# A new prologue for a fused attention and expert layer: order of loads, where the weights' means and low halves are made, and new order tables

## The reference, cut to what matters

```
n   = (x - mean_c x) / sqrt(var_c x + eps)                    # norm over channels, per pixel
qkv = Wqkv n                                                  # 256 -> 768 channels
agg = Wpw (depthwise 5x5 of qkv)                              # pointwise in groups of 8 channels
o   = relu linear attention, 8 channels a head, of qkv and of agg
y   = x + BN(Wproj o)                                         # 512 -> 256 channels
t   = (y - mean_c y) / sqrt(var_c y + eps)
w   = expert weights from softmax(router mean_t t), top 2
out = y + sum_e w_e (W2_e gelu(W1_e t + b1_e) + b2_e)         # 6 experts, 256 -> 341 -> 256
```

## Time and profile before

| what | us |
|---|---|
| median of 3 runs (1475.28 to 1476.71) | 1475.31 |
| the profiled execution | 1477.36 |
| its span, first to last instruction | 1475.3 |
| TensorE products busy | 1360.7 (92%) |
| VectorE busy | 1242.8 (84%) |
| ACT busy | 1059.0 (72%) |
| GpSimd busy | 973.3 (66%) |
| mean granted TensorE clock | 0.978 of full speed |

### The profile page before, as it was taken

How to read it: one execution, slowest core, us unless ns; L and a number is a source line. 1 busy time by engine, 2 the same in 40 slices (tenths; PEclk the granted TensorE clock), 3 DMA queues, 4 the chain that set the end, 5 groups by cost and what they waited for, 6 DMA issues and landing times. The chain is left out here.

```text
span 1475.3 us, 18697 instructions
## 1 busy us (share of the span) xinstructions
PE 1360.7 (92%) x6844; PEld 778.3 (53%) x6844; DVE 1242.8 (84%) x1273; ACT 1059.0 (72%) x1887; POOL 973.3 (66%) x736
## 2 busy tenths in 40 slices
PE   5897788799999999999999999999999998999998
...
DVE  2998799999999999999999999999999999960100
...
DMA packets 14250, 32.74 MB, mean 22 GB/s; under 512 B 2384, under 2 KB 5328, under 8 KB 13904
## 3 DMA queue, kind: packets, MB, share of 16 engines
...
...
## 5 line engine op out<-in xcount | busy, mean ns | idle before, releaser
L1125 DVE SCALAR_TENSOR_TENSOR dacc<-qkvs,dww,dacc 128x960 f32<-128x960 f32 (+4 forms) x930 | 1026.7, 1184 | 0.0
L969 POOL TENSOR_TENSOR gl<-hb,gh 128x512 f16<-128x512 f32 x256 | 307.6, 1204 | 261.0 <-ACT hb L735 257.9
L939 POOL TENSOR_TENSOR dwo<-dwo,tapb 128x992 f32<-128x992 f32 (+2 forms) x100 | 230.7, 2307 | 83.6 <-ACT tapb L709 45.1
L833 ACT ACTIVATE hb<-wbk,b1s 128x512 f32<-128x512 f32 x256 | 174.0, 682 | 88.5 <-PE wbk L504 83.8
L517 PE MATMUL acc<-gh,w2h 128*128 128x512 f16 x512 | 195.0, 381 | 7.7 <-POOL gl L969 6.0
L517 PE MATMUL acc<-gl,w2h 128*128 128x512 f16 x512 | 194.9, 381 | 0.0
L517 PE MATMUL acc<-gh,w2l 128*128 128x512 f16 x512 | 194.7, 380 | 0.0
L734 ACT ACTIVATE gh<-hb,ew 128x512 f16<-128x512 f32 x256 | 182.9, 714 | 0.8 <-PE acc L517 0.2
L735 ACT ACTIVATE hb<-hb,ew 128x512 f32<-128x512 f32 x256 | 182.2, 712 | 0.0
L504 PE MATMUL wbk<-th,w1h 128*128 128x512 f16 x512 | 153.2, 381 | 8.0 <-ACT hb L833 2.0
L504 PE MATMUL wbk<-th,w1l 128*128 128x512 f16 x512 | 152.9, 380 | 0.0
...
## 6 DMA issues: line engine op xcount, KB each, us to landing
...
dwo<-w SPq DMA_DIRECT2D x1, 2048.0 KB, 14.5
...
```

The costliest lines, as they stand in the source:

```text
L833: last = nc.scalar.activation(hb[:, f % GB, :], b[:], ACT.Gelu, bias=b1s[:, f % FT:f % FT + 1], scale=1.0 / (X_SCALE * W_SCALE))
L939: ins = nc.gpsimd.tensor_tensor(d3[:, oy, ox], d3[:, oy, ox], t3[:, iy, ix], ALU.add)
L969: nc.gpsimd.tensor_tensor(gl[:, f % GB, :], hb[:, f % GB, :], gh[:, f % GB, :], ALU.subtract).then_inc(g_low, 1)
L1125: ins = nc.vector.scalar_tensor_tensor(out=dst[:, oy, ox], in0=i3[:, jy, jx], scalar=dww[:, m, tap:tap + 1], in1=a3[:, oy, ox], op0=ALU.mu ...
```

## The change

It changes the prologue and all five order tables.

1. SP loads image 0 first, then Wqkv; W1 and the router follow behind the batch norm's small vectors, and W2 moves to the end of the list.
2. The means of Wqkv go to the `acc` banks, and TensorE no longer waits for their subtraction before it goes on.
3. The means of W1 are made in four pieces of 512 columns (`means.0.0` to `means.0.3`), with a matrix `mean_s` of 64/256, and VectorE centres and scales each piece in one instruction as it comes. They still stand behind the norm's row in the order. ACT casts W1 in two halves behind the first qkv evictions.
4. The low halves of W1 and W2 are made by GpSimd (`w1l`, `w2l`, two instructions each) from weights that are already scaled; for W2 ACT writes the scaled f32 copy, two more activations. They are no longer a condition for the first tap; TensorE, ACT and VectorE wait for them where they need the result or the space.
5. VectorE waits for the norm's row (`ln_chain`) before it makes the low half of Wqkv. The reciprocals stand ahead of the centring of W1, the mask of Wpw behind it.
6. ACT loads the table of Sqrt with a dummy instruction at the very start, and the roots of the batch norm stand ahead of `rbc`.
7. The matrices of tiles 4 and 5 lie in hb, those of 0 and 1 in yr[1]; the loads of x into yr[0] and yr[1] move with that.

```diff
@@ def schedule's table of image 0 (the four other tables are new too)
 FIRST = """
-squares.0.0.0 squares.0.0.1 weights.2 weights.0 sums.0.0 stats.0.0 rnorm.0.0 rbc.0.0.0 rbc.0.0.1 means.0
-apply.0.0.0 apply.0.0.1 high.0.0.0 low.0.0.0 weights.3 high.0.0.1 low.0.0.1 b weights.1 qkv.0.2.0 qkv.0.2.1
-qkv.0.3.0 qkv.0.3.1 qkv.0.4.0 matrices.0.4 qkv.0.4.1 qkv.0.5.0 qkv.0.5.1 squares.1.0.0 b qkv.0.0.0
-diag.0.4.0 matrices.0.5 matrices.0.0 diag.0.4.1 b squares.1.0.1 b diag.0.5.0 b sums.1.0 qkv.0.0.1 diag.0.5.1
...
+squares.0.0.0 squares.0.0.1 sums.0.0 wqh.0 stats.0.0 rnorm.0.0 roots.0 rbc.0.0.0 rbc.0.0.1 means.0.0
+means.0.1 means.0.2 means.0.3 apply.0.0.0 apply.0.0.1 high.0.0.0 low.0.0.0 high.0.0.1 low.0.0.1 qkv.0.2.0
+qkv.0.2.1 qkv.0.3.0 qkv.0.3.1 w1h.0.0 w1l.0.0 qkv.0.4.0 qkv.0.4.1 w1h.0.1 w1l.0.1 matrices.0.4 matrices.0.5
+qkv.0.5.0 squares.1.0.0 squares.1.0.1 diag.0.4.0 qkv.0.5.1 w2h.0.0 w2h.0.1 w2l.0.0 w2l.0.1 qkv.0.0.0
+diag.0.4.1 b b qkv.0.0.1 matrices.0.0 b b sums.1.0 qkv.0.1.0 diag.0.5.0 b diag.0.5.1 matrices.0.1 b
...
-AGG_PLACES = {1: (20, 25, 71, 79), 2: (18, 22, 74, 84), 7: (12, 22, 76, 82), 8: (19, 21, 75, 83)}
-RAW_PLACES = {0: (84, 87), 1: (61, 65), 2: (68, 70), 7: (67, 71)}
+AGG_PLACES = {1: (14, 19, 71, 77), 2: (19, 20, 80, 84), 7: (17, 20, 74, 83), 8: (19, 21, 75, 83)}
+RAW_PLACES = {0: (81, 82), 1: (58, 65), 2: (67, 71), 7: (67, 69)}
@@ sync
+            sp.dma_start(xa[:], x[0]...)                       # now first
             sp.dma_start(wqr, w_qkv...)
-            (w2 x2, w1, router, bn x3, w_proj, w_dw, w_pw x16, b2, b1, parts)
+            (bn x3, w1, router, w_dw, w_pw x16, w_proj, b2, b1, parts, w2 x2)
...
-                elif it == ("matrices", 0, 4):
-                    sp.wait_ge(weights_ready, 1)
+                elif it == ("w2l", 0, 1):
+                    sp.wait_ge(w2_low, 2)
                     sp.dma_start(yrs[0][:], ...)
-                elif it == ("diag", 0, 5, NCH - 1):
+                elif it == ("diag", 0, 1, NCH - 1):
@@ tensor
-            for dst, lo, hi in ((wbk[0][:, :], 0, CH), (wbk[1][:, 0:QKV - CH], CH, QKV)):
+            for dst, lo, hi in ((acc[:, 0, :], 0, CH), (acc[:, 1, 0:QKV - CH], CH, QKV)):
...
             last.then_inc(q_means, 1)
-            pe.wait_ge(q_centred, 4)
...
+                if s == 0 and f == 0:                          # in second()
+                    pe.wait_ge(w2_low, 2)
...
+                    for k in range(CT):                        # in means, for piece n = it[2]
+                        last = nc.tensor.matmul(af[:, n, :], mean_s[:], w1r[:, k, n * CH:(n + 1) * CH],
+                                                start=(k == 0), stop=(k == CT - 1))
+                    if n == FT * P // CH - 1:
+                        pe.wait_ge(q_centred, 4)
+                        (the router's means into acc[:, 0, 0:NP_])
                     last.then_inc(w1_means, 1)
...
+                            pe.wait_ge(w1_low, 2)              # first product of image 0
@@ scalar
+            act.wait_ge(mean_made, 1)
+            nc.scalar.activation(us[:, 0:1], mean_w[:, 0:1], ACT.Sqrt)
...
+                if what == "w1h":
+                    act.wait_ge(w1_centred, (FT * P // CH) * CT + CT)
+                    nc.scalar.activation(w1h[:, k], w1r[:, k], ACT.Copy).then_inc(w1_high, 1)
+                if what == "w2h":
+                    act.wait_ge(w2_loaded, 32)
+                    nc.scalar.activation(w2h[...], w2r[i], ACT.Copy, scale=W_SCALE)
+                    nc.scalar.activation(w2r[i], w2r[i], ACT.Copy, scale=W_SCALE).then_inc(w2_high, 1)
                 if what == "matrices":
-                    act.wait_ge(weights_ready, 1)
+                    act.wait_ge(w_loaded, 16 * (5 + HG))
+                    if m == DIAG_TILES[2]:
+                        act.wait_ge(w2_low, 2)
...
+                    if m < 4 and c == 0:                       # diag eviction
+                        act.wait_ge(w1_low, 2)
@@ gpsimd
+            nc.gpsimd.memset(mean_s[:], W_SCALE / C).then_inc(mean_made, 1)
...
+                    pool.wait_ge(w1_high, k + 1)
+                    nc.gpsimd.tensor_tensor(w1l[:, k], w1r[:, k], w1h[:, k], ALU.subtract).then_inc(w1_low, 1)
...
+                    pool.wait_ge(w2_high, i + 1)
+                    nc.gpsimd.tensor_tensor(w2l[:, tl], w2r[i], w2h[:, tl], ALU.subtract).then_inc(w2_low, 1)
@@ vector
             dve.wait_ge(q_high, 1)
+            dve.wait_ge(ln_chain[0], 4)
             (wql)
-            (w2l in two halves; mask of pw; W1 and router minus their means; reciprocals)
+            dve.wait_ge(bn_root, 2)
+            (reciprocals)
+            for n in range(FT * P // CH):
+                dve.wait_ge(w1_means, n + 1)
+                for k in range(CT):
+                    nc.vector.scalar_tensor_tensor(out=v, in0=v, scalar=W_SCALE, in1=af[:, n, :],
+                                                   op0=ALU.mult, op1=ALU.subtract).then_inc(w1_centred, 1)
+            (router minus its means; bnr, bnc; mask of pw; bnc; wp; pbias)
-            dve.wait_ge(w1_high, 1)
-            (w1l)
-            dve.wait_ge(w_split, 3)
             nc.vector.memset(rt[:], 0.0).then_inc(weights_ready, 1)
...
+                        if tap == LAST_TAP and s == 0 and pair == PAIRS[0]:
+                            dve.wait_ge(w1_low, 2)
```

More of the change, by code:

```diff
@@ L167 @@
-diag.0.0.1 apply.1.0.1 high.1.0.0 low.1.0.0 diag.0.1.0 tok.0.0 tok.0.1 b b b diag.0.1.1 high.1.0.1 b tok.0.2
-tok.0.3 b tok.0.4 tok.0.5 tok.0.6 low.1.0.1 b tok.0.7 relu_q.0.0 kv.0.0.0 kv.0.0.1 mask.0.0 relu_q.0.1
-att.0.0.0 att.0.0.1 att.0.0.2 att.0.0.3 scale.0.0.0 att.0.0.4 att.0.0.5 att.0.0.6 att.0.0.7 scale.0.0.1
-back.0.0.0.0 back.0.0.0.1 back.0.0.1.0 back.0.0.1.1 b agg.0.2.0 agg.0.2.1 agg.0.3.0 agg.0.3.1 qkv.1.2.0
-squares.2.0.0 qkv.1.2.1 squares.2.0.1 sums.2.0 qkv.1.3.0 qkv.1.3.1 b b b b stats.2.0 rnorm.2.0 b agg.0.4.0 b
@@ L179 @@
-qkv.0.0.1 qkv.0.1.0 G F back.-1.1.0.1 qkv.0.1.1 back.-1.1.1.0 F F back.-1.1.1.1 proj.-1.0.0 high.1.0.0
-low.1.0.0 high.1.0.1 b tok.0.0 proj.-1.0.1 tok.0.1 tok.0.2 tok.0.3 b low.1.0.1 tok.0.4 proj.-1.1.0 tok.0.5 b
-G proj.-1.1.1 F tok.0.6 S tok.0.7 S relu_q.0.0 squares.-1.1.0 squares.-1.1.1 sums.-1.1 kv.0.0.0 b kv.0.0.1
-stats.-1.1 mask.0.0 G relu_q.0.1 rnorm.-1.1 b att.0.0.0 att.0.0.1 S S att.0.0.2 att.0.0.3 F rbc.-1.1.0 F G
-rbc.-1.1.1 G apply.-1.1.0 G scale.0.0.0 att.0.0.4 att.0.0.5 S att.0.0.6 att.0.0.7 qkv.1.2.0 scale.0.0.1
@@ new lines @@
+mask.0.0 relu_q.0.1 stats.-1.1 S b rnorm.-1.1 b att.0.0.0 att.0.0.1 att.0.0.2 G att.0.0.3 G rbc.-1.1.0 F
+rbc.-1.1.1 apply.-1.1.0 apply.-1.1.1 scale.0.0.0 att.0.0.4 att.0.0.5 att.0.0.6 high.-1.1.0 qkv.1.2.0
+qkv.1.2.1 att.0.0.7 G scale.0.0.1 G F qkv.1.3.0 S high.-1.1.1 low.-1.1.0 low.-1.1.1 G logits.-1 back.0.0.0.0
+back.0.0.0.1 back.0.0.1.0 qkv.1.3.1 back.0.0.1.1 F S S S F S squares.2.0.0 exp.-1 agg.0.2.0 agg.0.2.1 F
+squares.2.0.1 agg.0.3.0 agg.0.3.1 sums.2.0 F b S G S stats.2.0 G G G F G S G b F F S S F rnorm.2.0 F S
@@ L196 @@
-back.-1.1.1.1 G b proj.-1.0.0 b tok.0.0 S G proj.-1.0.1 proj.-1.1.0 F tok.0.1 tok.0.2 tok.0.3 tok.0.4
-tok.0.5 low.1.0.1 b G tok.0.6 proj.-1.1.1 tok.0.7 relu_q.0.0 F squares.-1.1.0 squares.-1.1.1 kv.0.0.0
-kv.0.0.1 sums.-1.1 b F mask.0.0 relu_q.0.1 stats.-1.1 rnorm.-1.1 G att.0.0.0 att.0.0.1 S att.0.0.2 att.0.0.3
-rbc.-1.1.0 rbc.-1.1.1 G apply.-1.1.0 apply.-1.1.1 scale.0.0.0 F att.0.0.4 att.0.0.5 att.0.0.6 S G att.0.0.7
-scale.0.0.1 qkv.1.2.0 high.-1.1.0 qkv.1.2.1 F high.-1.1.1 qkv.1.3.0 low.-1.1.0 S low.-1.1.1 logits.-1 b
@@ new lines @@
+att.-1.1.3 scale.-1.1.0 att.-1.1.4 S b att.-1.1.5 att.-1.1.6 att.-1.1.7 scale.-1.1.1 F F b F G qkv.0.1.0
+qkv.0.1.1 S high.1.0.0 back.-1.1.0.0 low.1.0.0 back.-1.1.0.1 back.-1.1.1.0 back.-1.1.1.1 S G high.1.0.1
+low.1.0.1 F b G proj.-1.0.0 S tok.0.0 G proj.-1.0.1 b proj.-1.1.0 tok.0.1 S tok.0.2 tok.0.3 tok.0.4 b G
+tok.0.5 proj.-1.1.1 tok.0.6 tok.0.7 relu_q.0.0 F squares.-1.1.0 squares.-1.1.1 kv.0.0.0 kv.0.0.1 F sums.-1.1
+mask.0.0 relu_q.0.1 b stats.-1.1 att.0.0.0 att.0.0.1 rnorm.-1.1 G S att.0.0.2 att.0.0.3 rbc.-1.1.0
```

184 lines of the change are left out of this document (93 added, 91 removed).

## The result

The changed kernel takes **1442.57 us** (median of 4 runs, 1438.88 to 1444.24) beside 1476.01 for the kernel before (4 runs, 1475.28 to 1477.64): a ratio of 0.9769, 95% interval 0.9746 to 0.9791. The forecast of 1461.5 and its range of 1451.0 to 1470.5 were wrong: 33.4 us were won where 13.8 were expected. The profiled execution took 1441.29, 1.3 under the median, with a span of 1439.6 and a mean clock of 0.987.

The account below looks back on a forecast made before the run. TensorE and VectorE were taken as both full behind the prologue, so only an earlier start counted: 13.8 us from the prologue, 0 from the tables, 1475.31 - 13.8 = 1461.5 us; own range 1455 to 1468, wider range 1451 to 1470.5.

Parts of the forecast that it names:

- Loads and statistics: Start of prologue: Wqkv lands at about 7.9 us, statistics start at 12.5, eviction at 18.9; nothing gained up to here.
- The norm's row: Image 0's row takes 2.6 us instead of 7.9 with wql behind it; gain 5.3, spreading starts at about 21.8.
- the reciprocal beside the apply: VectorE's 1.74 us reciprocal beside GpSimd's apply costs 0; by the skill's rule, up to 1.7 us later.
- qkv and the first tap: Prologue: first qkv product at 33.4 instead of 38.56, VectorE's first tap at 37.5, 13.4 us earlier; tile 2 not the last.
- The list of what disappears: Ahead of the first tap: 4.4 us for w1l, 3.6 the cast, 5.2 the row, some three of the centring.
- Image 0: Attention wait 7 or 8 us instead of 2.86, image 1's centre-tap wait 2 to 3 instead of 6.99; first diag block 46.5.
- Rival C: Image 0's waits go as well: 10 of VectorE's 13.9 us of waits also won, about 1451 us; chance 0.11.
- The lead of the prologue: From image 1 on, VectorE and TensorE's chain both lead by 13.8 us; bounds 11 and 16.
- B: First tap moves but TensorE's chain does not follow, lead at the attention 5.8 us: 1469.5 us; chance 0.16.
- E: W1 lands at 35 instead of before 23.6 and holds qkv and the tap: 1473.5 us; chance 0.04.
- The tables of images 1 to 7: The new orders of the later images are worth 0, with 6 us kept on either side.
- Rival D: Slower: new tables make centre taps of later images wait for base adds, 2.7 us in each of seven: 1480.5; chance 0.07.

Follow-up runs that it names:

- experiment 9: The changed kernel with the loads in the old order (Wqkv, image 0, W2, W1, router, then the rest): 1443.47 us, ratio 0.9774 to the kernel before.
- experiment 8: The changed kernel without VectorE's wait for the norm's row ahead of Wqkv's low half: 1445.18 us, ratio 0.9782 to the kernel before.
- experiment 1: The changed kernel with the old order tables and places of images 1 to 8, prologue new: 1460.89 us, ratio 0.9895 to the kernel before.
- experiment 7: The changed kernel with W1's low halves back on VectorE ahead of its first tap: 1444.68 us, ratio 0.9792 to the kernel before.

## Why the prediction was wrong, point by point

- **Loads and statistics.** Wqkv landed at 7.76 (7.9 said). The eviction of the statistics came at 17.08, not 18.9, since they ran at the full clock (2.21 and 1.95 us for the two halves) where 18.9 had nearly all of them at half; they started at 13.04, 0.5 later than said, and the term was 1.8 too long. That the new loads gain nothing was right in the sum: the swap alone costs 2.2 us at the norm's row, and the earlier place of the batch norm's vectors gives them back (experiment 9).
- **The norm's row.** 2.6 us, as said, and for the reason said (experiment 8). The rule of the Trainium skill, SBUF — State Buffer, section on the two separate sides, that VectorE with two SBUF inputs and a GpSimd instruction that reads SBUF exclude one another, bears on this row, and the trace agrees (1.48 us for an instruction of 0.20). Where I weighed its other half, on the reciprocal beside the apply, I was right that the row costs nothing.
- **qkv and the first tap.** 31.34 and 34.75 against 33.4 and 37.5, the difference being the 1.8 of the statistics and about one us of VectorE's small work. What released the first tap was the eviction of tile 2 (0.43 us of wait), which I had said was not the last. The list of what disappears (4.4, 3.6, 5.2 and three) sums to 16.2 and not to its 13.4: ACT's cast of 3.6 lay beside VectorE's small work (42.77 to 46.39 and 42.65 to 46.41), so it can't be counted beside it. First diag block 44.30 against 46.5.
- **Image 0.** The wait for the attention 8.80 (7 or 8 said), that of the centre tap in image 1 2.26 (2 to 3), its start 169.42 (about 169). That these agree is in part luck: the chain stood 2.2 us ahead of its forecast at the first diag block and lost that again in image 0, where the first block alone took 8.46 us and not 6.6. Rival C is out: the waits did not go.
- **The lead of the prologue.** 13.8 said, bounds 11 and 16; by itself 15.3 in the span and 15.8 by medians. Right in mechanism, short by 1.5 to 2. The missing term is the length of the centre tap at 182.87, 3.30 us and then 1.29 (experiment 1), which I had in the upper bound only. The first tap is not what sets the prologue's worth (experiment 7). Rivals B and E are out.
- **The tables of images 1 to 7: this step failed.** I took 0, with 6 us on either side, and they are worth 15.5 alone and 18.3 on top of the prologue. What was there to win stood in my own text: TensorE idle 60.1 + 12.7 us. With prologue and tables it fell to 46.4 + 11.7, and over the whole span from 114.6 to 103.0 by the prologue alone, to 102.7 by the tables alone and to 87.3 by both. Two readings led me to 0. First, "TensorE and VectorE are both full, so neither can gain much": the busy share of VectorE, 96.5%, held some 20 us of waiting for GpSimd, told by a row of the page, centre taps of 1.82 us on average, where the ones at 112.59 and 174.59 took 1.29. My own rows had it at two places, 3.30 us for a centre tap in the earlier trace rows and 1.24 for GpSimd's mask in the earlier trace rows, and I used it for the mask alone. Second, I priced the tables by the largest wait of VectorE; but the costliest fault, that of the places (13.2 us on top of the new prologue and orders), was one that VectorE's waits can't show, its own short instruction standing too late for the others. Rival D had the sign wrong for the same reason.

Of the 18.3, image 1 has 8.4, images 2 to 6 have 7.1 and the end 4.2 (they overlap by 1.3). In a middle image's 2.4 us VectorE's waits have 1.9 and its busy time, exclusion included, 0.5, so there the exclusion is the smaller part. Which words of the new orders do this stays open: an order moves both.
